# A depthwise convolution with a routed product of eight experts: the lead expert chosen earlier, its loads moved, and 24 matmuls of zeros put first

## What is computed

```
y      = conv1d_depthwise_causal(x, taps) + b           # (8, 512, 1024)
idx    = argmax(y @ w_router.T)                          # (4096 tokens)
out    = x + (w_experts[idx] @ y)                        # only the chosen expert
```

## Time and profile before

| | us |
|---|---|
| median of three runs | 549.53 (548.73 to 549.76) |
| the profiled execution | 547.22 |
| its span, first to last instruction | 545.4 |
| PE busy | 509.8 (93%) |
| PE waiting for DVE's split of y, once | 12.7 |
| PE waiting for DVE's second copy of x, three times | 8.6 |
| PE waiting for the first loads of x, four times | 5.9 |

### The profile page before, as it was taken

One profiled execution on the slowest core, in us unless ns is written; L12 is line 12 of the kernel. 1 busy time (PEld: TensorE's weight loads), 2 busy tenths in 40 slices (PEclk: granted clock), 3 DMA queues, 4 the chain that ended last, 5 costly groups with the idle time before them and its releaser, 6 DMA issues.

```text
span 545.4 us, 9396 instructions
## 1 busy us (share of the span) xinstructions
PE 509.8 (93%) x2740; PEld 441.0 (81%) x2741; DVE 285.7 (52%) x376; ACT 151.4 (28%) x255; POOL 135.6 (25%) x148
## 2 busy tenths in 40 slices
PE   5999999876899945999999999999999999999995
PEld 5999999876688834888888888888888888888884
DVE  4945473464895105229976432295229422492761
ACT  2343434534200001006653100061006100160620
POOL 0004132070261102122233131222222222122312
PEclk9999999977899995999999999999999999999999
DMA  8977979996298995546999955479647964436344
GB/s 284 412 183 243 359 226 389 282 325 262 77 373 238 403 329 147 177 119 230 353 378 367 284 176 170 121 241 330 194 119 241 332 192 121 149 117 191 115 145 163
DMA packets 59477, 130.30 MB, mean 239 GB/s; under 512 B 12736, under 2 KB 32576, under 8 KB 59456
## 3 DMA queue, kind: packets, MB, share of 16 engines
q1 hardware_dynamic: 41840, 70.32, 41.6%
q0 software_dynamic: 14832, 54.27, 27.7%
q10 hardware_dynamic: 2784, 5.46, 3.4%
HBM read 94.56 MB, written 35.45 MB: 238 GB/s over the span
## 4 chain that ended last, share of the span: by engine, by line
PE 77%; DMA 11%; SPq 5%; issue 3%; DVE 2%; POOL 2%; ACT 0%; POOLq 0%; DVEq 0%
PE ps L817 61%; PE ps L775 15%; DMA xs<-x_t 6%; DMA ids_all<-y_sorted 3%; SPq L282 2%; DMA xs<-x_both 2%; SPq L382 2%; POOL y_sorted L873 1%; DMA y_sorted<-rows,pos_i 1%; DVE x_row L668 0%; SPq L304 0%; SPq L313 0%; DVE xs L498 0%; SPq L284 0%; SPq L294 0%
## 5 line engine op out<-in xcount | busy, mean ns | idle before, releaser
L817 PE MATMUL ps<-w_sb,ys 128*128 128x512 f32 x1680 | 385.7, 392 | 15.2 <-DVE ys L660 12.7
L817 PEld LDWEIGHTS ps<-w_sb,ys 128*128 128x128 f32 x1680 | 318.1, 190 | 82.2 <-issue 15.8
L775 PE MATMUL ps<-mats,xs 128*128 128x128 f32 x1024 | 123.8, 285 | 14.4 <-DVE xs L498 8.6
L655 DVE STREAM_TRANSPOSE y_cols<-y_blk 128x1024 f32<-128x1024 f32 x36 | 44.8, 1243 | 175.5 <-PE ps L817 144.7
L775 PEld LDWEIGHTS ps<-mats,xs 128*128 128x128 f32 x1024 | 122.0, 201 | 15.2 <-DVE xs L498 9.2
L434 ACT CAST ys<-y_cols 128x1024 fp32r<-128x1024 f32 x36 | 37.9, 1052 | 287.5 <-DVE y_cols L655 275.3
L885 POOL DMA_INDIRECT out<-x_row,idx x35 | 43.5, 1243 | 109.2 <-DVE x_row L668 106.4
L646 DVE TENSOR_TENSOR w_sb<-w_raw,w_sb 128x1024 fp32r<-128x1024 f32 x56 | 64.3, 1221 | 3.2 <-ACT w_sb L429 3.2
L429 ACT CAST w_sb<-w_raw 128x1024 fp32r<-128x1024 f32 x56 | 56.4, 1052 | 9.5 <-PE ps L817 8.4
L892 POOL COPY idx<-ids_all 128x1 int32 (+1 forms) x36 | 15.7, 436 | 172.6 <-DMA out<-x_row,idx 98.6
L873 POOL DMA_INDIRECT y_sorted<-rows,pos_i x32 | 36.3, 1134 | 82.6 <-PE ps L775 56.3
(11 more groups left out here) (95 smaller groups left out, 35.6 us busy)
## 6 DMA issues: line engine op xcount, KB each, us to landing
w_raw<-experts SPq DMA_DIRECT2D x56, 512.0 KB, 8.8
y_blk<-y_sorted SPq DMA_DIRECT2D x152, 128.0 KB, 2.6
xs<-x_both SPq DMA_DIRECT2D x15, 512.0 KB, 9.7
xs<-x_t SPq DMA_DIRECT2D x28, 256.0 KB, 6.3
xs<-x_t ACTq DMA_DIRECT2D x20, 256.0 KB, 6.2
w_first<-experts SPq DMA_DIRECT2D x8, 512.0 KB, 14.5
ids_all<-y_sorted SPq DMA_DIRECT2D x38, 1.0 KB, 3.5
x_row<-x_rows,idx POOLq DMA_INDIRECT x36, 4.5
```

Of the source, the lines that this page charges most:

```text
L655: V.transpose(y_cols[k][:, :, :].rearrange("p m (t i) -> p t m i", t=4), y_blk[:, k, :, :, :]).then_inc(y_blocks, 1)
L775: mm = nc.tensor.matmul(to, xs[:, n % X_RING, s % PACK, :], mats[:, s, :].rearrange("p (u n) -> p u n", n=SIDE), start=(s == sets[0]), sto ...
L817: mm = nc.tensor.matmul(out_ps[k][:, f * HALF:(f + 1) * HALF], ys[k][:, a, c, :], w_sb[:, c, b, f * HALF:(f + 1) * HALF], start=(c == 0 an ...
```

## The change

- `find_lead` runs after `place_rows(0)`, on the counts of one group. Its last step gives the row of slot 0 alone. `second_slot` (6 steps, after `place_rows(1)`) gives that of slot 1, and `third_slot` (5 steps) that of slot 2, cut to the tokens that are there.
- In each group DVE makes one second copy of x (k = 3) ahead of `place_rows` where it made four, and the lead expert's steps stand between `place_rows` and the next copy.
- The chunks of `w_first` are issued at packs 30, 34, ... 58, each behind the x of that pack, where they stood at packs 50 to 58.
- The y of slots 0 to 2 are issued behind all x loads.
- The y of slot 5 is issued between the two experts of `w_raw` instead of after both.
- `factors` is loaded in five pieces, the last three (packs 2 to 3, 4 to 7, 8 to 15) behind the x of packs 1, 3 and 5.
- DVE clears a tile `zeros`, and PE runs 24 matmuls of 128 by 128 of it in bf16 ahead of the convolution.

```diff
@@ -70,11 +70,11 @@
 
 
 LAST = GROUPS - 1
-FIRST = (LAST - 1) * GT // EXPERTS // P + 1
-MOST_SLOTS = (TOKENS + EXPERTS * (P - 1)) // P
+FIRST = 3
+MOST_SLOTS = FIRST + (TOKENS - P + EXPERTS * (P - 1)) // P
 RING = 2
-Y_AFTER = [(LAST + 1) * PACKS - 4, (LAST + 1) * PACKS - 2]
-ROUNDS = -(-(MOST_SLOTS + 1 - FIRST) // RING)
+W_AT = range(PACKS + X_RING + 6, GROUPS * PACKS, 4)
+ROUNDS = -(-(MOST_SLOTS - FIRST) // RING)
 SLOTS = FIRST + ROUNDS * RING + 3
 
@@ -88,8 +88,9 @@
 N_FACTORS = CH + SETS * (PHASES + EXPERTS)
-FACTOR_PACKS = [(0, 1), (1, 2), (2, 8), (8, PACKS)]
+FACTOR_PACKS = [(0, 1), (1, 2), (2, 4), (4, 8), (8, PACKS)]
 START_SETS = PACK // 2
+START_MATMULS = 24
 
 
 def constants():
...
@@ -336,36 +337,34 @@
             load_x(sp, 2)
             load_x(sp, 3)
             load_factors(3)
-            early = (LAST - 1) * PACKS + X_RING + 10
-            for n in range(4, early):
+            load_x(sp, 4)
+            load_x(sp, 5)
+            load_factors(4)
+            for n in range(6, GROUPS * PACKS):
+                if n == W_AT[0]:
+
+                    sp.wait_ge(lead_known, 1)
+                    e = sp.value_load(one_i[0:1, 0:1], min_val=0, max_val=EXPERTS - 1)
+
+                    sp.wait_ge(mats_ready, PACKS + 1)
                 if not on_second_queue(n):
                     load_x(sp, n)
-
-            sp.wait_ge(first_known, 1)
-            e = sp.value_load(one_i[0:1, 0:1], min_val=0, max_val=EXPERTS - 1)
-
-            sp.wait_ge(mats_ready, PACKS + 1)
-            chunks = iter(range(HC))
-            for k, n in enumerate(range(early, GROUPS * PACKS)):
-                if not on_second_queue(n):
-                    load_x(sp, n)
-                if k < 6 or k % 2 == 0:
-                    c = next(chunks, None)
-                    if c is not None:
-                        sp.dma_start(w_first[:, c, :], chunk(e, c)).then_inc(first_in[c], 16)
-                if n in Y_AFTER:
-                    t = Y_AFTER.index(n)
-
-                    sp.wait_ge(y_out[t], TPG * 16)
+                if n in W_AT[:HC]:
+                    c = W_AT.index(n)
+                    sp.dma_start(w_first[:, c, :], chunk(e, c)).then_inc(first_in[c], 16)
+
+            for t in range(FIRST):
+
+                sp.wait_ge(lead_known, t + 1)
+                row = lead_row(t)
+
+                sp.wait_ge(y_out[t % 2], (t // 2 + 1) * TPG * 16)
+                if t < RING:
+
                     sp.wait_ge(w_split, t + 1)
-                    load_y(sp, lead_row(t), t, ids_all[:, t:t + 1, :])
-
-            sp.wait_ge(third_known, 1)
-            row = lead_row(2)
-
-            sp.wait_ge(y_out[0], 2 * TPG * 16)
-            sp.wait_ge(y_blocks, 1)
-            load_y(sp, row, 0, ids_all[:, 2:3, :])
+                else:
+                    sp.wait_ge(y_blocks, t - 1)
+                load_y(sp, row, t % RING, ids_all[:, t:t + 1, :])
 
             sp.wait_ge(rows_ready, 1)
             sp.wait_ge(y_out[1], 2 * TPG * 16)
@@ -380,9 +379,10 @@
                     e = sp.value_load(load_i[0:1, k:k + 1], min_val=0, max_val=EXPERTS - 1)
                     for c in range(HC):
                         sp.dma_start(w_raw[k][:, c, :], chunk(e, c)).then_inc(raw_in[k][c], 16)
-
-            sp.wait_ge(y_blocks, FIRST + 1)
-            load_slot(FIRST + 2, (FIRST + 2) % RING)
+                if k == 0:
+
+                    sp.wait_ge(y_blocks, FIRST + 1)
+                    load_slot(FIRST + 2, (FIRST + 2) % RING)
             replace_raw(FIRST, loads)
             last = sp.value_load(one_i[0:1, 3:4], min_val=0, max_val=ROUNDS - 1)
             with sp.Fori(0, ROUNDS) as i:
@@ -396,7 +396,7 @@
 
         @block.scalar
         def _(act):
-            act.wait_ge(warm_zero, 1)
+            act.wait_ge(warm_zero, 2)
             nc.scalar.activation(warm[:, 1:2], warm[:, 0:1], ACT.Identity)
 
             act.wait_ge(x_in[0], 16)
@@ -479,6 +479,7 @@
         @block.vector
         def _(dve):
             V = nc.vector
+            V.memset(zeros[:, :], 0.0).then_inc(warm_zero, 1)
             V.memset(warm[:, :], 0.0).then_inc(warm_zero, 1)
 
             def build_mats(first, n):
@@ -562,15 +563,27 @@
                 step(V.tensor_copy(one_i[:, 0:1], one[:, 0:1]))
                 step(V.tensor_tensor(tmp, lead, const(C_BASE), ALU.mult))
                 step(V.tensor_reduce(full_row, tmp, AX.X, ALU.add))
-                V.tensor_scalar(lead_i[:, 0:2], const(C_SPLIT, 2), full_row, None, ALU.add).then_inc(first_known, 1)
+                V.tensor_copy(lead_i[:, 0:1], full_row).then_inc(lead_known, 1)
+
+            limit = one[:, 6:7]
+
+            def next_slot(most):
+
+                step(V.tensor_tensor(count, base, const(C_BASE), ALU.subtract))
+                step(V.scalar_tensor_tensor(out=done, in0=count, scalar=most, in1=lead, op0=ALU.min, op1=ALU.mult))
+                step(V.tensor_reduce(limit, done, AX.X, ALU.add))
+                step(V.tensor_scalar(one[:, 7:8], limit, full_row, -float(P), ALU.add, ALU.add))
+                return one[:, 7:8]
+
+            def second_slot():
+
+                row = next_slot(float(2 * P))
+                step(V.tensor_scalar(limit, limit, float(P), None, ALU.add))
+                V.tensor_copy(lead_i[:, 1:2], row).then_inc(lead_known, 1)
 
             def third_slot():
 
-                step(V.tensor_tensor(count, base, const(C_BASE), ALU.subtract))
-                step(V.scalar_tensor_tensor(out=done, in0=count, scalar=float(FIRST * P), in1=lead, op0=ALU.min, op1=ALU.mult))
-                step(V.tensor_reduce(one[:, 6:7], done, AX.X, ALU.add))
-                step(V.tensor_scalar(one[:, 6:7], one[:, 6:7], full_row, -float(P), ALU.add, ALU.add))
-                V.tensor_copy(lead_i[:, 2:3], one[:, 6:7]).then_inc(third_known, 1)
+                V.tensor_copy(lead_i[:, 2:3], next_slot(limit)).then_inc(lead_known, 1)
 
             def count_slots():
                 many = cmp[:, :, :, :].rearrange("p a s e -> p (a s e)")[:, 0:EXPERTS * TILES].rearrange("p (e t) -> p e t", e=EXPERTS)
@@ -691,21 +704,21 @@
                 for k in range(3):
                     double(n + k)
                 choose(g - 1)
-                for k in range(3, 7):
-                    double(n + k)
+                double(n + 3)
                 place_rows(g - 1)
-                double(n + 7)
-                if g < LAST:
-                    if g == LAST - 1:
-                        find_lead()
-                    for k in range(8, PACKS):
-                        double(n + k)
+                if g == 1:
+                    find_lead()
+                elif g == 2:
+                    second_slot()
                 else:
                     third_slot()
-                    for c in range(4):
-                        low(0, c, w_first)
-                        double(n + 8 + 2 * c)
-                        double(n + 9 + 2 * c)
+                for k in range(4, 8):
+                    double(n + k)
+                for k in range(8, PACKS, 2):
+                    if g == LAST:
+                        low(0, k // 2 - 4, w_first)
+                    double(n + k)
+                    double(n + k + 1)
                 if g < LAST:
                     sum_most(g)
 
@@ -792,6 +805,9 @@
                                           start=False, stop=(t == TPG - 1), skip_group_check=True)
                 mm.then_inc(ranked, 1)
 
+            pe.wait_ge(warm_zero, 1)
+            for n in range(START_MATMULS):
+                nc.tensor.matmul(ps[:, 7, 0:P], zeros[:, :], zeros[:, :], start=True, stop=True, skip_group_check=True)
             for g in range(GROUPS):
                 for s in range(SETS):
                     if g and s == 3 * PACK:
```

More of the change, by code:

```diff
@@ L202, in build @@
         warm = sb("warm", [P, 2])
+        zeros = sb("zeros", [P, P], BF16)
         part = sb("part", [P, 2, LOGITS, BANKS])
@@ L255, in build @@
         route_step = sem("route_step")
-        first_known = sem("first_known")
-        third_known = sem("third_known")
+        lead_known = sem("lead_known")
         rows_ready = sem("rows_ready")
```

## The result

The changed kernel has a median of **533.86 us** over four runs (532.54 to 536.02), the kernel before beside it 549.51 (548.73 to 549.76). The ratio is 0.9721 with a 95% interval of 0.9688 to 0.9755: 15.7 us faster. The forecast was 529.2, 20.3 faster, with a range of 521 to 537. The profiled execution took 532.54 us, with a span of 530.7 (545.4 before).

What follows compares the result with a forecast made beforehand. PE, busy for 93% of the span, was taken as the bound, with losses at the start, in the last group and at slot 5. Terms summed to -20.3 us, from 549.5 to 529.2, range 521 to 537.

Steps and rivals of the forecast that it cites:

- slot 6: Before slot 6 of the products: its y lands late, PE waits, +2.9 us (1.6 to 4.2); slow matmuls follow, +1.5.
- the hand-over: Between convolution and products: PE waits about 2.1 us instead of 2.55, term -0.45 (-2.5 to +2).
- the fourth group: Last convolution group: weights backlog and y ahead of x go, with three waits and slow matmuls, -14.4 us.
- the factors: Start of the convolution: fewer bytes ahead of the x of packs 2 and 4, -1.1 us (0 to -1.3).
- the clock behind the wait ahead of pack 20: Third group: slow matmuls follow PE's new wait of 2.6 there, +1.7 us (0 to +3.0).
- the three new waits: Ahead of packs 20, 36 and 52 PE waits for the second copy of x: +2.6, +1.4 and +1.2 us.
- Zeros: Ahead of pack 0: the matmuls of zeros gain nothing because loads decide the start, 0 us (0 to -1.7).
- section (b): Last group in the kernel before: 17.2 us lost; the y of slot 0 holds SP's queue ahead of x.
- Slot 5: Before slot 5 of the products: its y lands near 185, so wait and slow clock go, -12.7 - 2.9 us.
- Weights starving x in the scatters: Rival, during scatters: x behind weight chunks lands late, PE waits 1.6 us each time; +8, 537 us; chance 0.15.
- The fourth group did not keep its waits: Rival, last convolution group: two longer waits and slow matmuls stay, 12.7 us, so 542 us; chance 0.08.
- Slot 5 or 6 waiting as before: Rival, in the products: loads share one bandwidth and only change places; +11, so 540 us; chance 0.07.

Runs made afterwards that it cites:

- the repeat: The changed kernel itself, with nothing altered, run again in the third set: 534.09 us (ratio 0.9748).
- the run with three copies: The changed kernel, but DVE makes three second copies of x ahead of place_rows in each group instead of one: 529.71 us (ratio 0.9674).
- the kernel with the held scatter: The changed kernel, but POOL scatters the third group's y only when the y of slots 0 and 1 has landed: 538.28 us (ratio 0.9824).
- the run with the second expert behind it: The changed kernel, but the second expert of w_raw is loaded behind the y of slot 6: 527.63 us (ratio 0.966).
- the run with both edits: The changed kernel with three copies of x ahead of place_rows and w_raw's second expert behind the y of slot 6: 522.71 us (ratio 0.9542).

## Why the prediction was right, and where its sizes were off

The direction, the places and the range were right; the gain was 15.7 of 20.3 forecast. In the profile the terms below add up to 15.3 less, and the span became 14.7 shorter. That the total lies in the range is in part luck: against the forecast some terms were together 7.6 too favourable (slot 6, the hand-over, the fourth group, the factors) and others 2.7 too unfavourable (the clock behind the wait ahead of pack 20, and the three new waits). Point by point, by the steps of the prediction:

**Zeros: 0, right.** Pack 0 ran in 2.05 in the first profile, and the time did not move, because pack 2 waits for loads and matrices. The Trainium skill, TensorE: Matmul & The Clock Gate, Part 1, has the slow clock as the default that activity releases. The 2.02 to 2.06 of three executions agree with it; the 2.58 to 3.75 of the seven others with the same zeros show that these 24 matmuls often did not suffice.

**Factors: -1.1, measured -0.84** (pack 19 began at 42.53 before and at 41.69 after). That is one execution of each. In the eight profiled executions with a wait behind pack 19 it began between 41.65 and 42.70, and no run has this part of the change alone. In the first profile the bound is DVE's matrices of pack 2, which wait for their piece of `factors`; in others, the repeat among them, it is the x load. I had named the load of x alone.

**The waits behind place_rows: +2.6, +1.4 and +1.2, measured 2.02, 1.16 and 1.03.** I had taken `find_lead` at 2.40 with one step of 0.47, and that step took 0.23 this time. And I had counted the pack ahead of the wait at 1.80, where PE is busy for 2.03 up to the end of its last record. The mechanism is shown by the run with three copies. The term of 1.7 for the clock was 0 in the first profile and 1.62 in the repeated one: the size was right, and it is paid in some executions.

**The fourth group: -14.4, measured about -13.0** (23.07 for 192 records leaves 1.45, of which 1.02 is a stall in which the profile names no releaser; the repeat has 21.70 and so all of the 14.4). The sum was right and its reasoning only in part: section (b) called the y load ahead of x the cause. That holds for the wait of 4.23, which is gone when y alone moves. But this gives 1.3 us only, since the other waits stay (3.27 and 2.33) and the hand-over's grows to 7.72. With weights in a row x lands after 19.8 us without any y ahead of it, and that costs 6 us.

**The hand-over: a wait of 2.1, measured 4.51, and 5.84 in the repeat.** Here 2.4 us went. The step that failed is that the wait for slot 0's y was put at nothing. DVE waited 1.03 for it in the first profile and 2.43 in the repeat. By the runs this y is the bound: with x earlier the wait grows to 4.19 and the time stays, and without the scatter it is gone. I had named the possibility and put no price on it. It stood beside the rule of the Trainium skill (DMA: Bandwidth & Descriptors, Queues, rings and completion order) that a DMA engine takes whole packets in turn; that rows of 1 KB get less by it was my own conclusion. Of the first profile's 2.4 the wait for y is 1.0, and 1.2 is its last copy of x, which ended at 124.7 and not at 123.5. So a second step was off as well: the time of the last x load, "issued when pack 55 is done". ACT issues it behind the eviction of a bank of seven sets, six of which belong to pack 56. That makes 1.6 us: in the kernel with the held scatter, whose fourth group starts at 106.25, pack 55 ends near 113.5 and the load leaves ACT at 115.05. In the first profile it left at 117.21; the other 2.1 come with the stalls of this execution, whose cause is open, and not from the kernel's order.

**Slot 5: -12.7 - 2.9, right, by luck of a small margin.** Its y was forecast for 185 with products from 141, that is 44 us after their start. It landed at 186.0 with products from 133.87, 52 us after. The split ended at 189.6, and slot 4 at 190.2, so about half a us was to spare and not 8. Three executions of other kernels have waits of 0.35, 0.95 and 1.99 there. The error was the rate and, more, the bytes. I counted eight chunks (4.2 MB) at 403 GB/s and 2.6 us for the y behind them. From the first chunk's issue to this landing (164.72 to 186.0) the DMAs moved 7.21 MB at a mean of 339 GB/s, since y of other slots, gathered and scattered rows and the next expert's chunks move in the same time. At 403 the 7.21 MB would have taken 17.9 us, so of the 8 us some 3.4 are the rate and the rest are bytes that I left out. The stretches of the changed kernel show the rate (length, five engines, PEclk, DMA share, GB/s):

```profile
174.00:177.00 3.00, 3.00 (x15) 2.49 (x14) 0.00 (x0) 0.00 (x0) 1.23 (x2) 1.00 1.02 411
178.00:181.00 3.00, 3.00 (x15) 2.49 (x14) 0.00 (x0) 0.00 (x0) 0.25 (x1) 1.00 1.10 252
186.00:190.00 4.00, 4.00 (x20) 3.30 (x19) 3.58 (x3) 1.05 (x1) 0.86 (x2) 1.00 1.02 412
...
207.00:212.00 5.00, 5.00 (x14) 3.84 (x13) 2.73 (x3) 1.04 (x1) 0.70 (x2) 0.50 0.77 232
```

At 178 to 181 full DMAs carry 252 GB/s, and 411 before and 412 after it. The packets of that stretch are small ones, and only SP's queue has any:

```profile
DMA packets 648, 0.76 MB, mean 252 GB/s; under 512 B 129, under 2 KB 575, under 8 KB 648
```

That these are the y of slot 5 is concluded from the 1 KB rows and from its place behind the eight chunks.

**Slot 6: +2.9 and +1.5 for the clock, measured 5.03 and about 2.9** (207 to 212 at 1.2 GHz in the stretches above, from 206.26 on). It landed 68.6 us after the first product, forecast 66.6. This term was too small by 3.5, the largest miss (2.0 for the later landing, 1.4 for the clock), though its mechanism was the one that the run with the second expert behind it shows. With 5.65 in the repeat the wait came close to the 6 us that I had named as a sign of being wrong.

**The rivals.** Weights starving x in the scatters of the second and third group did not happen: their last 240 records take 27.07, without a wait. The fourth group did not keep its waits. Slot 5 or 6 waiting as before came half true: 5.03 of 12.70.

## What to carry to other kernels

A load is not late only because of what stands ahead of it in its queue. Compare its landing with all bytes asked for in the same stretch, and try the order and the bytes apart. Of a transfer that moves ahead of another, work out when the next one lands, with the rates of its own row size. And of a load issued by an engine that also computes, take the time of the instruction it stands behind, not that of the buffer it needs.

## What the runs showed of the hardware that I had not expected

- The same wait of 2.02 us was followed by 3.4 us at 1.2 GHz in three of eight profiled executions and by none in five. The length of a wait did not decide it in other places either: waits of 2.33 (y ahead of x) and 2.45 (weights in a row) were followed by 1.2 GHz, and waits of 2.54 (held scatter), 2.69 (y of slot 5 alone) and 3.27 (y behind x) were not. The prediction had gone by the length of four waits (1.40 and 1.48 against 2.55 and 2.87).
- In the changed kernel's first profile DVE stands 1.42 us before 114.42 and PE 1.02 before 116.89 with "issue" as the only releaser, and ACT 2.38 before 117.03. Shorter gaps of PE of this kind stand in the fourth group without zeros (0.39, 0.91, 0.94), with three copies (0.22, 0.27) and with the second expert behind slot 6 (0.32, 0.24), and none in the repeat or in the run with both edits. Their cause stays open.
- While most packets are of under 2 KB (575 of 648 at 178 to 181 us), the DMAs carry 252 GB/s at full share, and 411 beside it. In the kernel before it is 205 GB/s at 198 to 202, with 625 of 706 packets under 2 KB.
